# A graph network's second edge layer: where the fifth fetched tile's names are compared, and one turn of three that fetches four tiles

## The reference

```python
ss, vv = (s[src], v[src])                       # one row of 160 numbers for every edge
out0 = C0 * (ss * e0 @ W1 + dot * INV3 @ W2)
p3 = (ss @ W3)[:, :, None] * e1[:, None, :] * INV3
p4 = jnp.einsum('eui,uw->ewi', vv * e0[:, :, None], W4) * INV3
p5 = jnp.einsum('eui,uw->ewi', jnp.cross(vv, e1[:, None, :]), W5) * INV6
m_agg = jax.ops.segment_sum(m, dst, num_segments=n)
return x + jax.nn.relu(h_out)                   # h_out: m_agg through Ws and Wv
```

## Time and profile before

| | |
|---|---|
| median of 3 runs | 1931.6 us (1929.72 to 1934.15) |
| the profiled execution's own time | 1932.38 us |
| its span | 1930.6 us |
| TensorE matmul busy | 1743.2 us, 90% |
| VectorE busy | 1610.8 us, 83% |
| GpSimd busy (the 0.3 us between gathers are not counted) | 1423.8 us, 74% |
| ScalarE busy (the issue of DMAs is not counted) | 180.1 us, 9% |
| mean granted TensorE clock | 0.961 |
| moved by DMA | 181.05 MB, 94 GB/s |

### The profile page before, as it was taken

One profiled execution on the slowest core, in us unless ns is written; L12 is line 12 of the kernel. 1 busy time (PEld: TensorE's weight loads), 2 busy tenths in 40 slices (PEclk: granted clock), 3 DMA queues, 4 the chain that ended last, 5 costly groups with the idle time before them and its releaser, 6 DMA issues.

```text
span 1930.6 us, 57886 instructions
## 1 busy us (share of the span) xinstructions
PE 1743.2 (90%) x16272; PEld 1517.5 (79%) x16272; DVE 1610.8 (83%) x2961; ACT 180.1 (9%) x390; POOL 1423.8 (74%) x1439
## 2 busy tenths in 40 slices
PE   8989898989888888899975999999999999999997
PEld 6667676767767676667645999999999989999897
DVE  7888787878787878878888998988888888988886
ACT  5100000010010100000032000000000000000000
POOL 4677777777777777777755777777777777777774
PEclk9899999999999999999976999999999999999998
DMA  8344343444343433333323332323232232322323
GB/s 268 107 104 106 104 106 104 106 105 105 94 115 95 105 104 105 105 104 105 103 65 96 78 75 72 76 66 77 69 75 75 69 79 67 78 71 75 76 69 92
DMA packets 110507, 181.05 MB, mean 94 GB/s; under 512 B 30328, under 2 KB 74992, under 8 KB 110016
## 3 DMA queue, kind: packets, MB, share of 16 engines
q0 software_dynamic: 67440, 115.19, 24.8%
q1 hardware_dynamic: 35592, 59.07, 9.8%
q10 hardware_dynamic: 7112, 2.94, 0.7%
HBM read 170.04 MB, written 7.05 MB: 92 GB/s over the span
## 4 chain that ended last, share of the span: by engine, by line
PE 44%; POOL 21%; issue 12%; ACTq 9%; DVE 8%; DMA 3%; ACT 2%; DVEq 1%; POOLq 0%
POOL g L848 21%; PE sums L1204 10%; ACTq L733 8%; PE sums L1190 8%; PE w_ps L1158 7%; PE w_ps L1215 6%; PE hid_ps L1144 5%; PE sums L1225 4%; DVE match L996 2%; PE sums L1194 2%; DMA g<-node_table 1%; ACTq L730 1%; DMA g<-node_table,src 1%; ACT arena L874 1%; DVE arena L1042 1%
## 5 line engine op out<-in xcount | busy, mean ns | idle before, releaser
L848 POOL DMA_INDIRECT g<-node_table,src x1394 | 1398.1, 1003 | 452.3 <-issue 409.2
L1215 PE MATMUL w_ps<-split,match 128*128 128x320 f32 x3600 | 565.4, 315 | 6.1 <-DVE match L996 6.0
L1215 PEld LDWEIGHTS w_ps<-split,match 128*128 128x128 f32 x3600 | 538.2, 190 | 7.1 <-DVE match L996 7.1
L996 DVE TENSOR_TENSOR match<-hid_ps,node_id_sb 128x3200 fp32r<-128x3200 f32 x116 | 399.0, 3459 | 7.7 <-ACT hid_ps L894 7.5
L1042 DVE TENSOR_TENSOR arena<-w_ps,g 128x384 f32<-128x384 f32 (+3 forms) x693 | 298.2, 458 | 54.7 <-PE w_ps L1158 38.4
L1158 PE MATMUL w_ps<-fc_sb,arena 64*128 64x224 f32 x1612 | 223.6, 384 | 96.0 <-ACT arena L874 54.6
L1194 PE MATMUL sums<-g,sel 128*128 128x160 f32 x1612 | 247.8, 303 | 42.8 <-DMA g<-node_table,src 34.8
L1190 PEld LDWEIGHTS sums<-arena,sel 128*32 128x32 f32 x6448 | 200.3, 112 | 107.1 <-issue 68.6
L1158 PEld LDWEIGHTS w_ps<-fc_sb,arena 64*128 64x128 f32 x1612 | 173.2, 195 | 129.9 <-DVE arena L1036 76.8
L968 DVE TENSOR_TENSOR sel<-mixed,sh 128x896 f32<-128x896 f32 x232 | 251.7, 1085 | 26.9
L1194 PEld LDWEIGHTS sums<-g,sel 128*128 128x128 f32 x1612 | 227.1, 190 | 54.1 <-issue 25.9
(11 more groups left out here) (108 smaller groups left out, 699.4 us busy)
## 6 DMA issues: line engine op xcount, KB each, us to landing
g<-node_table SPq DMA_DIRECT2D x2304, 0.6 KB
g<-node_table ACTq DMA_DIRECT2D x2304, 0.6 KB
arena<-edge_feat_dram SPq DMA_DIRECT2D x60, 512.0 KB
g<-node_table,src POOLq DMA_INDIRECT x1394
named<-src_rows_dram SPq DMA_DIRECT2D x30, 320.0 KB
X<-x_dram SPq DMA_DIRECT2D x5, 400.0 KB, 6.6
named<-src_rows_dram SPq DMA_DIRECT2D x30, 64.0 KB
sh<-edge_sh_dram SPq DMA_DIRECT2D x1, 1624.0 KB
```

The lines of the kernel that those rows point to most:

```text
L848: nc.gpsimd.indirect_dma_start(out=g[:, slot(p, u, j), :], out_offset=None, in_=table[layer], in_offset=bass.IndirectOffsetOnAxis(ap=src[: ...
L996: nc.vector.tensor_tensor(match[MATCH_OF[i]][:], wanted_of[i].unsqueeze(1).to_broadcast(wide), node_id_sb[:].unsqueeze(2).to_broadcast(wid ...
L1215: last = nc.tensor.matmul(banks[:, BANK_OF[i], 0:2 * D], match[MATCH_OF[i]][:, t, :], split[:, t, :], start=(t == 0), stop=(t == NT - 1))
```

## The change

Two edits, both in layer two. First, the fifth tile's numbers are still cast by ScalarE into `arena`, but ahead of the comparison VectorE now copies them into `wanted` (the 128 columns of `mixed`, in PSUM), waits on a new semaphore `late_copied`, and compares from there. Second, in the turns of p = 0 (`SPARSE`) the pick of index 1 (`SPARED`), tile 5 of group 1, is not fetched: its comparison, find and join fall away, GpSimd gathers that tile, and the pick behind it counts the semaphores up by 2.

```diff
+SPARSE, SPARED = 0, 1
...
-        wanted_of = [early_named[:, i, :] for i in range(EARLY)] + [late_named]
+        wanted_of = [early_named[:, i, :] for i in range(EARLY)] + [wanted]
...
-            def picks_at(o, s, ahead):
+            def picks_at(o, s, p, it, ahead):
 
                 u, nxt = (o + ahead) % UNROLL, (o + ahead) // UNROLL
                 if s is not None and s + ahead >= GROUPS:
                     return []
-                return [(i, nxt) for i in range(NP) if PICKS[i][0] == u]
+                q = turn_after(p, it) if nxt else p
+                return [(i, nxt, q) for i in picked(q) if PICKS[i][0] == u]
+
+            def picked(p):
+                return [i for i in range(NP) if not (p == SPARSE and i == SPARED)]
+
+            def turn_after(p, it):
+                return (p + 1) % PERIOD if p >= 0 else 0 if it == LEAD - 1 else -1
...
+            def weight(p, i):
+                return 2 if p == SPARSE and i == SPARED + 1 else 1
...
-                        others |= {j for v, j in PICKS if v == u}
+                        others |= {PICKS[i][1] for i in picked(p) if PICKS[i][0] == u}
...
                     wide = [P, NT, P]
+                    if i >= EARLY:
+                        nc.vector.tensor_copy(wanted, late_named).then_inc(late_copied, 1)
+                        dve.wait_ge(late_copied, f + (nxt + 1))
                     nc.vector.tensor_tensor(match[MATCH_OF[i]][:], wanted_of[i].unsqueeze(1).to_broadcast(wide),
                                             node_id_sb[:].unsqueeze(2).to_broadcast(wide),
-                                            ALU.is_equal).then_inc(match_done, 1)
+                                            ALU.is_equal).then_inc(match_done, weight(q, i))
...
-                        if not own_weights and (o % UNROLL, j) in PICKS:
-                            pe.wait_ge(found_copied, NP * f + (PICKS.index((o % UNROLL, j)) + 1))
+                        if not own_weights:
+                            for i in picked(p):
+                                if PICKS[i] == (o % UNROLL, j):
+                                    pe.wait_ge(found_copied, NP * f + (i + 1))
...
-                    last.then_inc(found, 1)
+                    last.then_inc(found, weight(q, i))
```

More of the change, by code:

```diff
@@ L650, in edge_layer @@
             late_cast = sem(L + "late_cast")
+            late_copied = sem(L + "late_copied")
             match_done = sem(L + "match_done")
@@ L983, in match_rows, with compare @@
                                             ALU.is_equal).then_inc(match_done, 1)
-                def compare(f, i, nxt, s):
+                def compare(f, i, nxt, q, s):
                     if not exists(i, s):
@@ L989, in compare @@
                         dve.sem_inc(match_done, 1)
+                        dve.sem_inc(late_copied, 1)
                         return
@@ L995, in compare, with join @@
                     wide = [P, NT, P]
+                    if i >= EARLY:
+                        nc.vector.tensor_copy(wanted, late_named).then_inc(late_copied, 1)
+                        dve.wait_ge(late_copied, f + (nxt + 1))
                     nc.vector.tensor_tensor(match[MATCH_OF[i]][:], wanted_of[i].unsqueeze(1).to_broadcast(wide),
                                             node_id_sb[:].unsqueeze(2).to_broadcast(wide),
-                                            ALU.is_equal).then_inc(match_done, 1)
-                def join(f, p, i, nxt, s):
+                                            ALU.is_equal).then_inc(match_done, weight(q, i))
+                def join(f, i, nxt, q, s):
                     if not exists(i, s):
@@ L1008, in join @@
                     dve.wait_ge(found, NP * f + (NP * nxt + i + 1))
-                    nc.vector.tensor_reduce(g[:, slot(p, u, j), :], banks[:, BANK_OF[i], 0:2 * D].rearrange("p (h c) -> p c h", h=2),
-                                            AXX, ALU.add).then_inc(found_copied, 1)
+                    nc.vector.tensor_reduce(g[:, slot(q, u, j), :], banks[:, BANK_OF[i], 0:2 * D].rearrange("p (h c) -> p c h", h=2),
+                                            AXX, ALU.add).then_inc(found_copied, weight(q, i))
                 def products(f, it, o, h, s, p, e):
@@ L1085, in stage @@
                             for u in range(2):
-                                for i, nxt in picks_at(0, s, u):
-                                    compare(f, i, nxt, s + u)
+                                for i, nxt, q in picks_at(0, s, p, it, u):
+                                    compare(f, i, nxt, q, s + u)
                     live = s is None or s < GROUPS
@@ L1095, in stage @@
                         if s == 0:
[L1096 to L1101, removed]
+                            for i, nxt, q in picks_at(o, s, p, it, 0):
+                                join(f, i, nxt, q, s)
+                        for i, nxt, q in picks_at(o, s, p, it, 2) if live else []:
+                            compare(f, i, nxt, q, None if s is None else s + 2)
+                        for i, nxt, q in picks_at(o, s, p, it, 1) if live else []:
+                            join(f, i, nxt, q, None if s is None else s + 1)
                     if live:
@@ L1205, in find0, with find @@
                     last.then_inc(found, 1)
-                def find(f, i, nxt, s):
+                def find(f, i, nxt, q, s):
                     if not exists(i, s):
@@ L1234, in stage @@
                             pe.wait_ge(split_ready, 1)
[L1235 to L1238, removed]
+                            for i, nxt, q in picks_at(o, s, p, it, 0):
+                                find(f, i, nxt, q, s)
+                        for i, nxt, q in picks_at(o, s, p, it, 1) if s is None or s < GROUPS else []:
+                            find(f, i, nxt, q, None if s is None else s + 1)
                     elif o == 1:
```

## The result

| | before | changed |
|---|---|---|
| median | 1931.96 us (4 runs, 1929.72 to 1934.15) | 1876.91 us (4 runs, 1873.47 to 1878.49) |
| ratio | | 0.9713 (95%: 0.9694 to 0.9731) |
| span of the profiled execution | 1930.6 us | 1876.3 us |

Faster by 2.9%, 55 us. The forecast was 1890, 42 us less than before: the sign and the mechanism were right, the gain was 13 us larger than said.

A forecast was written before the change was run, and what follows sets the result against it. POOL (GpSimd) was taken to set the pace at 91.5 us a period; a new period of 86.6 saves 36.9 us in 26 intervals, the interval before 3.3, the tail 0.5: 40.7 off 1932.4 gives 1891.7, said as 1890, range 1875 to 1906.

The forecast's parts named there:

- the first rival: Layer two: copy hidden everywhere, smaller clock loss, period down to POOL's (GpSimd's) 85.0 us, total 1876; chance 0.13.
- the 0.31 us of the copy: VectorE, ahead of the fifth comparison: the added copy costs 0.31 us in each turn that VectorE paces.
- GpSimd set the pace and the comparison held it: Layer two: GpSimd's period of 91.6 us sets the pace, each comparison from `arena` costing it 2.6 us.
- The copy does not shut GpSimd out: Copy into PSUM: holds no gather; the opposing rival said 1.1 us a turn, 1901, sharing a chance of 0.17.
- The turns: Layer two, between `lin2` starts: 25.4 us from p = 2 to 0, 28.8 from 0 to 1, 32.45 from 1 to 2.
- the sum of the new period: Layer two: three turns, taken from the early ones, add up to 86.6 us, above POOL's 85.0.
- The last two intervals: End of layer two: one interval of p = 0 to 1 at 28.8 us, one of p = 1 to 2 at 32.45.
- The tail: End of the kernel: the last gathers come earlier, an estimated 0.5 us less.
- The interval before the eight periods: Layer two, the interval of 28.12 us before 1111.00: loses 3.3 us, to 24.8 by VectorE.
- ScalarE's queue in the short turn: Turn of 25.4 us: ScalarE's copy, casts and 24 + 24 rows take 24.3 us, fitting by 1.1.
- a sign of being wrong: Profile after: ScalarE's rows of a turn ending behind the next `lin2` would show the forecast wrong.
- The spared fetch frees nothing: Rival, short turn: the 3.4 us return as another wait, period 90.4 us, total 1925; chance 0.08 up to 1928.

The follow-up runs named there:

- the rows moved: Changed kernel with eight of ScalarE's row DMAs moved from the turn of p = 1 to p = 0: 1867.99 us, ratio 0.9670.

## Why the prediction was right, and where its size was off

**Where the result lies.** 1876.91 us is in the stated range of 1875 to 1906, but only 2 us from its lower end and below the 1882 to 1897 that the forecast held likeliest. It is in the band of the first rival, 1873 to 1882, which had 0.13. That rival had two conditions. The first, that the 0.31 us of the copy are hidden everywhere, came true. The second, that GpSimd's pace of 85.0 us then takes over, did not: the period is the sum of the three turns, 85.44 us, and one gather less a turn changes nothing. That the two periods are only 0.4 us apart, and the total so near the rival's 1876, is luck as far as the runs show.

**GpSimd set the pace and the comparison held it: right.** The first edit takes all long gathers away, the second alone brings nothing, a second such comparison costs 70 us. It was one bound with two edits behind it: the first alone is worth 21 us, the second alone costs 4, both together are worth 53 (1878.35 against 1930.9). By themselves the nine spared finds are worth 32 us only once GpSimd is free.

**The copy does not shut GpSimd out: right,** none of 630 gathers over 980 ns, among them those that start inside a copy. The Trainium skill's "SBUF — State Buffer", section "Who interferes with whom", warns of copies, and the Trainium skill's "VectorE: DVE Perf Modes", section "Why PSUM operands drop a tier", takes that back for an operand in PSUM; the trace agrees with the second, 0.95 us for the gather at 1451.71.

**The turns: right in their pattern, 25.4, 28.8 and 32.45 predicted, 24.9, 28.48 and 32.04 measured in the mean.** Eight periods were to take 8 x 86.6 = 692.8 us and took 683.5: 9.3 us of the 13 that the forecast missed. The step that was mis-sized is the sum of the new period, in three terms:

- The copy was charged with 0.31 us in two turns of three. It costs nothing, and neither do two; four add 0.56 us to the turn of p = 0. "VectorE goes from one transpose to the next in 28.42 us without an idle gap worth a name" was read too quickly: there was about 1 us ahead of the accumulation, in which the engine waits for its own sequencer, and that gap closes when VectorE is late. The forecast named these small gaps in its first rival and gave that 0.13.
- The turn from p = 2 to p = 0 was started from 28.83 us, the one such turn at hand in the early stretch. With five tiles and a free GpSimd the steady value is 28.55, as the first edit alone shows.
- The turn from p = 1 to p = 2 was given the 32.45 us of one early turn whose finds were slowed. Seven of eight such turns now take 32.1 to 32.45 us, and one, whose finds are not slowed, takes 30.54. That is 3.3 us of the 9.3.

By themselves the three make 5.0, 2.2 and 3.3 us; 1.2 us came back, since the turn from p = 2 to p = 0 takes 24.92 us in the mean and not 28.55 - 3.78 = 24.77.

**The last two intervals: another 3.8 us.** They were given a loop turn's 28.8 and 32.45 us and take 28.13 and 29.30 (the starts of `lin2` above, 1789.05 to 1846.48). In the last period, which is written out and not in the loop, the wait for the rows is 0.92 us and the finds behind it are not slowed:

```profile
1836.87 0.54 PE L1213 MATMUL sums<-g,sel 128*128 128x160 f32 x2 [0.92 <-DMA g<-node_table]
1837.14 7.61 PE L1234 MATMUL w_ps<-split,match 128*128 128x320 f32 x50
```

**The ends** nearly cancel. The tail was to be 0.5 us shorter and is 1.2 longer (from 28.65 to 29.8 us from the last full turn's `lin2` to the end), and layer two began 1.8 us earlier in this execution; other executions of the same kernel differ by as much (1081.10 and 1083.79 us for the same `lin2`). The interval before the eight periods was to lose 3.3 us and lost 3.7 (28.12 to 24.46): there TensorE's find counts, and not VectorE's work.

**ScalarE's queue in the short turn: it does not quite fit, without harm.** The forecast saw a margin of 1.1 us, and called it the thinnest. The timeline (start us, us, and what it waited for):

```profile
1439.98 10.48 ACTq L746 DMA_DIRECT2D g<-node_table  x24
1453.20 0.38 ACT L893 ACTIVATE lin_sb<-sums 80x256 f32<-80x256 f32 x1 [14.43 <-issue]
```

The rows end at 1450.46, behind the start of `lin2` at 1448.54, which the prediction had named as a sign of being wrong; and `lin2`'s result, ready by 1450.9, is copied at 1453.20 only. In seven of the eight short turns inside the loop this copy is 2.0 to 2.5 us late, and before the change none is. No engine is seen to wait for it between 1200 and 1800 us, and the next one, at 1479.40, is on time again. "The spared fetch frees nothing" did not come about.

## What to carry to other kernels

When two engines run in step, find out which one has the lead and by how much before a wait is priced: a bound that is taken away shows the next one at once, here at 85.4 us a period behind 91.5, and with the rows moved 82.1. An engine that waits for nothing but "issue" still has slack if its sequencer does loads there. Where GpSimd gathers, look for a long `tensor_tensor` of VectorE with both operands in SBUF: here a copy of 0.27 us that put one of them in PSUM paid for itself. And a cost of a few us can hide in the spread of the clock: compare the turns, not the totals alone.

## What the runs showed of the hardware

- A `tensor_tensor` of 3.45 us with both inputs in SBUF makes one of GpSimd's indirect gathers 2.45 to 2.7 us longer on average (28 and 57 cases): the first that starts inside it, which then ends 0.82 us behind it, while one that already runs keeps its 0.95 us. With the small operand in PSUM it doesn't, and a copy of 0.27 us from SBUF to PSUM doesn't either. The Trainium skill's "SBUF — State Buffer", section "Who interferes with whom", has the rule for two SBUF inputs against an instruction that reads SBUF, and infers that the writing of descriptors itself isn't held by it. Here the gather was held; these gathers also read their row numbers (`src`) from SBUF. No run told the two apart.
- TensorE's clock behind a short wait falls or does not, for the same wait. In the changed kernel the two finds behind the rows (start us, us) and the granted clock of the two stretches:

```profile
1412.47 0.75 PE L1213 MATMUL sums<-g,sel 128*128 128x160 f32 x2 [2.26 <-DMA g<-node_table]
1412.82 2.54 PE L1234 MATMUL w_ps<-split,match 128*128 128x320 f32 x8
...
1668.87 0.54 PE L1213 MATMUL sums<-g,sel 128*128 128x160 f32 x2 [2.15 <-DMA g<-node_table]
1669.13 3.05 PE L1234 MATMUL w_ps<-split,match 128*128 128x320 f32 x19
```

```profile
core 0: us, PE busy (x) PEld busy (x) DVE busy (x) ACT busy (x) POOL busy (x), PEclk, DMA share, GB/s
1412.80:1421.90 9.10, 9.10 (x54) 9.10 (x54) 7.35 (x9) 0.00 (x0) 6.87 (x8) 0.82 0.27 64
1669.10:1676.70 7.60, 7.60 (x53) 7.60 (x53) 7.14 (x9) 0.00 (x0) 5.77 (x7) 1.00 0.27 67
```

9.1 us at a granted 0.82 (part of that stretch at 1.2 GHz instead of 2.4) in seven of the nine periods, 7.60 at 1.00 in the other two; with four copies it was slow in two of nine. That is worth 1.5 us a period and may account for much of the spread of the runs: of the changed kernel's eight executions the one with the highest mean granted clock, 0.968, took 1869.22 us, those at 0.954 took 1877.85 and 1878.84 (one at 0.960, though, took 1883.25). What decides it stays open.
- A comparison with the names in `mixed` takes 3.49 us in the mean of 28, with those in `hid_ps` 3.45 (the changed kernel has 107 of these).
